# Attention scores of a macaron block on Trainium2: two PSUM banks per slot, or three banks with one head of the next slot computed early

## The reference

```python
def _L0_attn_ref(x, WQ, WK, WV, WO):          # x: (16, 256, 128), 16 heads, D_K = 8
    Q, K, V = (heads(WQ), heads(WK), heads(WV))
    score = jnp.einsum('bhqd,bhkd->bhqk', Q, K) / jnp.sqrt(jnp.asarray(D_K, x.dtype))
    score = score + mask                       # -inf above the diagonal
    score = score - jnp.max(score, axis=-1, keepdims=True)
    score = jnp.exp(score)
    score = score / jnp.sum(score, axis=-1, keepdims=True)
    out = jnp.einsum('bhqk,bhkd->bhqd', score, V)
    ...
    return out @ WO
...
x = x + 0.5 * _L0_ffn_ref(_layernorm(x, axis=-1), L0_ffn_gate_w, L0_ffn_w1, L0_ffn_w2, L0_ffn_w3)
x = x + _L0_attn_ref(_layernorm(x, axis=-1), L0_attn_WQ, L0_attn_WK, L0_attn_WV, L0_attn_WO)
x = x + 0.5 * _L0_ffn_ref(_layernorm(x, axis=-1), L0_ffn_gate_w, L0_ffn_w1, L0_ffn_w2, L0_ffn_w3)
```

## Time and profile before

| | |
|---|---|
| median of 3 runs | 566.49 us (564.69 to 567.13) |
| profiled execution | 565.05 us, its span 563.0 us |
| granted TensorE clock, mean | 0.993 of full speed |
| busy time of PE, DVE, ACT, POOL | 501.2, 373.7, 317.2, 267.9 us |
| score products (L1753) | 1024, mean 244 ns each |
| score maxima (L1322) | 128, mean 816 ns each |
| exponentials (L953) | 128, mean 813 ns each |

### The profile page before, as it was taken

How to read it: one execution, slowest core, us unless ns; L and a number is a source line. 1 busy time by engine, 2 the same in 40 slices (tenths; PEclk the granted TensorE clock), 3 DMA queues, 4 the chain that set the end, 5 groups by cost and what they waited for, 6 DMA issues and landing times.

```text
span 563.0 us, 19023 instructions
## 1 busy us (share of the span) xinstructions
PE 501.2 (89%) x7286; PEld 411.0 (73%) x7286; DVE 373.7 (66%) x995; ACT 317.2 (56%) x597; POOL 267.9 (48%) x325
## 2 busy tenths in 40 slices
PE   1689999999999788898889886888889999999995
PEld 1679998988889456565656554655579999999995
DVE  5656865324675789999898898776375532455665
ACT  4945654433335576767676765667744444445553
POOL 7967877612463323333431111565607601666662
PEclk9999999999999799999999999999999999999999
DMA  9971247786764314846212120311147755843222
GB/s 271 306 242 50 61 100 161 175 157 155 129 138 121 102 59 108 245 109 186 79 58 62 41 60 2 119 57 36 45 94 164 155 133 130 156 119 91 72 75 56
DMA packets 114661, 65.86 MB, mean 117 GB/s; under 512 B 51856, under 2 KB 108432, under 8 KB 114576
## 3 DMA queue, kind: packets, MB, share of 16 engines
q1 hardware_dynamic: 84400, 38.95, 27.0%
q0 software_dynamic: 6912, 14.17, 10.0%
q10 hardware_dynamic: 23264, 11.54, 8.3%
HBM read 18.88 MB, written 34.87 MB: 95 GB/s over the span
## 4 chain that ended last, share of the span: by engine, by line
PE 61%; DVE 20%; ACT 6%; DMA 5%; issue 4%; POOL 1%; SPq 1%; ACTq 0%; DVEq 0%; POOLq 0%
PE bank L1641 19%; PE bank L1522 10%; PE bank L1524 10%; PE bank L1523 10%; DVE negmax L1322 8%; ACT pt L953 3%; PE bank L1753 3%; PE bank L1534 2%; PE bank L1816 2%; PE bank L1783 2%; DMA yg<-sorted_y,row 2%; DVE X L1219 2%; PE bank L1831 1%; ACT r_xn L785 1%; ACT ot L933 1%
## 5 line engine op out<-in xcount | busy, mean ns | idle before, releaser
L689 POOL DMA_INDIRECT yg<-sorted_y,row x108 | 104.1, 964 | 141.7 <-PE bank L1641 45.7
L1210 DVE SCALAR_TENSOR_TENSOR pt<-bank,pt 128x512 f32<-128x512 f32 x122 | 84.3, 691 | 118.3 <-PE bank L1524 109.8
L953 ACT ACTIVATE pt<-bank 128x768 f32<-128x768 f32 x128 | 104.1, 813 | 72.2 <-PE bank L1792 71.7
L675 POOL DMA_INDIRECT sorted_x<-xs,row x108 | 106.5, 987 | 52.0 <-issue 22.5
L1641 PE MATMUL bank<-w,pt 128*128 (+1 forms) x976 | 130.0, 277 | 0.0
L1641 PEld LDWEIGHTS bank<-w,pt 128*128 128x128 f32 x976 | 118.6, 192 | 3.2
L1322 DVE TENSOR_REDUCE negmax<-bank 128x10 f32<-128x640 f32 x128 | 104.4, 816 | 17.1 <-PE bank L1770 15.3
L829 ACT ACTIVATE pt<-bank 128x512 f32<-128x512 f32 x122 | 72.8, 597 | 26.3 <-PE bank L1524 25.1
L837 ACT ACTIVATE yb<-bank 128x256 f32<-128x256 f32 x82 | 31.5, 384 | 79.5 <-PE bank L1641 72.9
L1753 PE MATMUL bank<-zc 63*64 63x64 f16 (+3 forms) x1024 | 43.0, 244 | 16.6 <-DVE negmax L1322 13.8
L1753 PEld LDWEIGHTS bank<-zc 63*64 63x64 f16 x1024 | 18.9, 105 | 43.6 <-DVE negmax L1322 29.3
(11 more groups left out here) (171 smaller groups left out, 1015.8 us busy)
## 6 DMA issues: line engine op xcount, KB each, us to landing
sorted_y<-yb ACTq DMA_DIRECT2D x82, 128.0 KB
sorted_x<-zeros SPq DMA_DIRECT2D x2, 2944.0 KB, 14.5
zc<-qk_rows SPq DMA_DIRECT2D x84, 64.0 KB
qk_rows<-qksplit SPq DMA_DIRECT2D x8, 512.0 KB, 2.8
sorted_x<-zeros SPq DMA_DIRECT2D x1, 2432.0 KB, 11.4
sorted_x<-zeros SPq DMA_DIRECT2D x1, 2176.0 KB, 10.3
X<-x_in SPq DMA_DIRECT2D x8, 256.0 KB, 5.1
zc<-w_up SPq DMA_DIRECT2D x8, 256.0 KB, 6.7
```

The lines of the kernel that those rows point to most:

```text
L675: ps.indirect_dma_start(out=sorted_x[s], out_offset=bass.IndirectOffsetOnAxis(ap=row[:, s, k, t:t + 1], axis=0), in_=xs[:, R0[s] + t, :], ...
L689: ps.indirect_dma_start(out=yg[:, a % D_YG, k, :], out_offset=None, in_=sorted_y[s], in_offset=bass.IndirectOffsetOnAxis(ap=row[:, s, k, t ...
L953: s_.activation(pt[:, hg, (u % 2) * 768:(u % 2 + 1) * 768].rearrange("p (a n) -> p a n", a=2), bank[:, B_ST:B_ST + 2, 0:384], ACT.Exp, sca ...
L1210: v_.scalar_tensor_tensor(hid[:, n % D_HID], bank[:, B_H3 + n % 2, :], 1.0 / WSCALE, silu[:, n % D_H], ALU.mult, ALU.mult).then_inc(prod_d ...
```

## The change

PE no longer writes the scores of a slot ahead in one piece. Three banks, 0, 1 and 2, hold scores; an even slot uses 0 and 1, an odd one 1 and 2. The transposed scores move from banks 2 and 3 to banks 3 and 4. The head whose bank the slot before does not use (`first_side`: head 0 in bank 0 for an even slot, head 1 in bank 2 for an odd one) is computed one slot earlier, behind the transposed scores (`score_first`); the other head, in bank 1, is computed where both were before (`score_second`). In the first slot of attention both stand together. Each part has four products and two masks, all on the two quarters of the array of one head. The loop over heads is taken out of the products, so that in the early slots, too, the four products of head 0 stand ahead of the four of head 1. The numbers of instructions and DMAs are the same, those of the other engines and their order too, except that VectorE's reduction reads banks 0 and 1 or banks 1 and 2.

```diff
-        B_S, B_ST, B_O = 0, 2, 5
+        B_S, B_ST, B_O = 0, 3, 5
...
+        def score_place(n, a):
+
+            return B_S + n % 2 + a
+
+        def first_side(n):
+
+            return n % 2
+
...
-            def row_max(b, q, k, b0=B_S):
+            def row_max(b, q, k, early=False):
+                n = PAIRS * b + k
+                b0 = B_EARLY if early else score_place(n, 0)
...
-            def score_products(b, q, u, G_z=None, b0=B_S):
+            def score_products(b, q, u, a, place, G_z=None):
...
-                pe.wait_ge(s_reduced, freed(PAIRS * b + u))
                 for n in range(2):
-                    for a in range(2):
-                        rows = slice(HALF * a, HALF * (a + 1) - 1)
-                        for g in range(2):
...
+                    rows = slice(HALF * a, HALF * (a + 1) - 1)
+                    for g in range(2):
...
+            def score_masks(a, place):
+
+                own = causal[side(a), :, HALF * a:HALF * (a + 1)]
+                for g in range(2):
+                    parts = bank[side(g), place, 0:S_COLS].rearrange("p (s k) -> p s k", k=HALF)
+                    last = t_.matmul(parts[:, g:PARTS:4 - g, :], one(a), own,
+                                     start=False, stop=True, skip_group_check=True)
+                return last
+
+            def score_first(b, q, u, G_z):
+
+                n = PAIRS * b + u
+                if n > PAIRS + AHEAD:
+                    pe.wait_ge(s_reduced, done(n - 2, D_S))
+                a = first_side(n)
+                score_products(b, q, u, a, score_place(n, a), G_z)
+                score_masks(a, score_place(n, a))
+
+            def score_second(b, q, u):
+
+                n = PAIRS * b + u
+                if n > PAIRS + AHEAD:
+                    pe.wait_ge(s_reduced, done(n - 1, D_S))
+                a = 1 - first_side(n)
+                score_products(b, q, u, a, score_place(n, a))
+                score_masks(a, score_place(n, a)).then_inc(s_ready, 1)
...
                     if ahead is not None:
-                        score_products(*ahead, G + 1 if ahead[1] % 2 == 0 else None)
-                        score_masks()
+                        if b == 0 and u == 0:
+                            score_first(*ahead, None)
+                        score_second(*ahead)
                     score_t_products(b, q, u)
                     score_t_masks()
+                    coming = score_bank(b, q, u + 1) if u + 1 < PAIRS else score_bank(b + 1, q + 1, 0)
+                    if coming is not None:
+                        score_first(*coming, coming[0] // 2 if coming[1] % 2 == 0 else None)
...
-                    score_products(slot // PAIRS, slot // PAIRS, slot % PAIRS, 0 if slot < PAIRS else None, B_EARLY)
-                    score_masks(B_EARLY)
+                    pe.wait_ge(s_reduced, freed(slot))
+                    for a in range(2):
+                        score_products(slot // PAIRS, slot // PAIRS, slot % PAIRS, a, B_EARLY + a,
+                                       0 if slot < PAIRS and a == 0 else None)
+                    for a in range(2):
+                        last = score_masks(a, B_EARLY + a)
+                    last.then_inc(s_ready, 1)
```

More of the change, by code:

```diff
@@ L1453, in first_groups @@
                 if slot is not None:
-                    row_max(slot // PAIRS, slot // PAIRS, slot % PAIRS, B_EARLY)
+                    row_max(slot // PAIRS, slot // PAIRS, slot % PAIRS, early=True)
                 if slot == PAIRS - 1:
@@ L1762, in one @@
                 return ident_b[side(a), side(a)]
-            def score_masks(b0=B_S):
-                for a in range(2):
-                    own = causal[side(a), :, HALF * a:HALF * (a + 1)]
-                    for g in range(2):
-                        parts = bank[side(g), b0 + a, 0:S_COLS].rearrange("p (s k) -> p s k", k=HALF)
-                        last = t_.matmul(parts[:, g:PARTS:4 - g, :], one(a), own,
-                                         start=False, stop=True, skip_group_check=True)
-                last.then_inc(s_ready, 1)
+            def score_masks(a, place):
[19 more added lines that the diff above has]
+                score_masks(a, score_place(n, a)).then_inc(s_ready, 1)
             def score_t_products(b, q, u):
```

12 lines of the change are left out of this document (6 added, 6 removed).

## The result

| | before | changed |
|---|---|---|
| median, same chip | 565.76 us (4 runs, 564.69 to 567.13) | 572.28 us (4 runs, 570.94 to 572.83) |
| profiled execution | 565.05 us, span 563.0 | 571.94 us, span 569.9 |
| granted TensorE clock, mean | 0.993 | 0.997 |

The ratio is 1.0123, 95% interval 1.0091 to 1.0156: slower by 1.2%, 6.5 us between the medians. The forecast was 571.5 us, with 565.5 to 578.5 and a chance of 0.65 for slower.

What follows compares the result with a forecast made beforehand. PE bounds the first FFN; in attention mostly VectorE, some slots PE. Terms 1.0 + 3.0 + 1.7 + 0.4 = 6.1 us on 565.05 give 571.2, stated as 571.5 us; range 565.5 to 578.5.

Steps and rivals of the forecast that it cites:

- the early slots: Twelve blocks between expert units: head 1's short products wait behind head 0's long ones, 0.08 us each, 1.0 us in all.
- the waits for the DMAs: Attention, slot u = 3 of every second sequence: `score_first` waits for `zc` ahead of projection and transposes, 1.7 us in all.
- array time of one head alone, a slot: Behind the transposed scores, `score_first` adds its own time on PE: 0.19 us for each of 116 slots.
- attention slots, with VectorE's other waits: Attention: `score_first` delays reach VectorE in 13 slots plus remainders, 3.0 us; the reciprocal's later transposes add 0.4 us.
- wait for the DMAs, last group: Last group: PE waits for `zc` first, projection and transposes follow, 1.1 us plus the part's own 0.2, 1.3 us.
- the same, fourth group: Fourth group: up to 1.1 us of new waiting for `zc`, partly hidden by VectorE's work; 0.4 us taken.
- Columns per quarter, not a price per matmul: Score blocks on the array: time follows columns on each quarter, so one head lasts as long as both, 0.22 us.
- the halves that end no sooner: `score_second` behind the wait: masks still start 0.16 us after its first product, VectorE 0.45 us after it; gain 0.
- Covered in most slots: Attention: PE's waits, ScalarE's copy or VectorE's other work hide most 0.19 us parts; 13 slots and remainders cost 3.0 us.
- VectorE's waits don't fall: Attention: VectorE's waits for score masks, 23 times and 11.1 us, should not shrink.
- The rival of a maximum that starts sooner: Attention: a shorter part behind the wait halves VectorE's 11.1 us of waiting, giving 561 us; chance 0.07.
- PE as the bound: Attention: parts costing 0.3 us exceed the cover and PE drags most slots, giving 580 us; chance 0.12.

Runs made afterwards that it cites:

- opposite halves and no early wait: Changed kernel with odd slots' banks swapped and a new half group's first head not sent ahead: 566.39 us, ratio 1.004 to the kernel before.
- opposite halves: Changed kernel with odd slots' banks swapped, so head 0 is always sent ahead: ratios to the kernel before 0.998, 0.9983 and 0.9946, all on slower chips.
- doubled part: Changed kernel with every `score_first` (four products, two masks) issued twice in a row: 580.38 us, ratio 1.0312 to the kernel before.

## Why the prediction was right

The forecast held, and its mechanism, the columns of each quarter and a wait moved ahead of other work, is the measured one. Of its terms, some were mis-sized and offset one another, and that the sum came out as close as it did is luck: the early slots were 0.9 us too high and the waits for the DMAs 1.2 too low. The two executions that were profiled also differ by 1.5 us ahead of the first maximum, in code that is the same. To separate them I compare the changed kernel with the last one above, opposite halves and no early wait: both traces have the same clock at the start of attention, which the kernel before's has not. The stretch in which attention starts, of before and, in the second fence, of opposite halves with no early wait:

```profile
182.00:195.00 13.00, 10.41 (x203) 6.81 (x201) 7.88 (x23) 7.22 (x12) 4.63 (x6) 0.74 0.42 113
```

```profile
184.00:197.00 13.00, 9.01 (x201) 6.71 (x203) 8.82 (x27) 7.45 (x12) 4.50 (x6) 1.00 0.47 135
```

The granted clock was 0.74 in one and 1.00 in the other, as in the changed kernel. Counted from the first of each, the 33rd maximum of before comes 0.6 us later than in the other trace and the 33rd exponential 0.85 us later. From first to last exponential the changed kernel takes 5.65 us more than opposite halves with no early wait.

| term | forecast | measured |
|---|---|---|
| array time of one head alone, a slot | 0.19 | 0.192 |
| early slots | 1.0 | 0.1 |
| attention slots, with VectorE's other waits | 3.0 + 0.4 | 2.8 |
| wait for the DMAs, last group | 1.3 | 2.2 |
| the same, fourth group | 0.4 | 0.65 |
| sum | 6.1 | 5.7 |

The measured terms of attention are steps in the distance between the maxima of the two kernels: 0.65 at the fourth group, 2.2 at the last, the rest in single steps of up to 0.3 us. They are a little small, since the kernel compared with still pays 0.2 to 0.5 us itself; against before at an equal clock attention grew by 5.9 to 6.1 us.

- *Columns per quarter, not a price per matmul* was right, by 0.192 us, by the halves that end no sooner, and by opposite halves, which fit beside one another. It also says what the alternative was: the other head's quarters stood empty beside each part. The working on record was weaker than its result: 160 ns for eight products, 60 for four masks and 170 for eight transposed products are 20, 15 and 21 ns each, which rules out a fixed price per matmul only by the masks. The doubled part does it: six matmuls on two quarters take the time of twelve on four. The Trainium skill's rule of about 81 ns for a matmul of 128 columns ("TensorE: Matmul & The Clock Gate", section "Back-to-back issue gap") does not hold for these quarters: an estimate by it gives the doubled part, six more pairs, 0.49 us, and it took 0.21. The page gives this figure for a stream of pairs and says nothing of quarters or places. The full products of 128 columns don't show it either, each with a weight load of its own: they stand 0.06 us apart (302.70 and 302.76 in the earlier trace rows).
- *The early slots* are the step that failed: "dispatch is in order: the long products of head 0 wait for the short ones on their quarters before head 1 may begin". They don't hold head 1 back: its short product starts 0.014 us after that of head 0, and the twelve blocks cost 0.08 us together in place of 1.0. In the changed slot above, too, a matmul of a free quarter starts ahead of one that stands before it in the program and waits for its own quarter. The price was also set too high in itself, since 64 to 128 columns at 2.4 GHz are 0.03 to 0.05 us and not 0.05 to 0.08. The same page of the Trainium skill says under "Step-by-step: what each phase is for" that matmuls stay in program order; for the starts on different quarters the trace disagrees (305.37 ahead of 305.39).
- *Covered in most slots* was right. 13 fully exposed slots and remainders were counted, 3.0 us, and the waits behind them 0.4; 2.8 were measured. The doubled part came out at 3.8 times the single one in slots 66 to 96, as going through the slots had given it. Over all of attention it did not: the doubled kernel takes 15.1 us more than opposite halves with no early wait, with the waits for the DMAs adding nothing, where 12.5 had been counted. That its whole time fell in the expected range is luck, since the lost wait offset this.
- *The wait for the DMAs* was right in place and too small in size. I had counted the projection and the transposes behind it, and 0.2 for the part; but nothing lies beside a part that waits by itself (0.32), VectorE's normalisation comes late too (0.16), and the transfer itself took 0.66 us longer from its issue than in the trace that I read.
- *VectorE's waits don't fall*, 11.1 us in both. The rival of a maximum that starts sooner is out. PE as the bound is out as well: it is found waiting for VectorE 60 times still.

What stays open: why the change costs nothing that can be measured on the slower chips. In slots 66 to 96 it costs the same 1.25 us there, so the array time is paid. One term is absent there: all waits for the DMAs between 195 and 400 us in the unedited changed kernel's trace are

```profile
PE bank L1761 <- DMA zc<-qk_rows: 0.4, 1, 0.4
```

and from the maximum of slot 111 to that of slot 112 are 1.93 or 1.94 us in it and in every other trace from such a chip. SP's issue stands 7.7 us ahead of the maximum of slot 111 there (381.40 and 389.10). So the last group's 2.2 us are not paid. That leaves some 3.5 us of the table unaccounted for. The rest of attention is full of gaps that belong to no wait, behind which a late part may be hidden, but no trace of the kernel before was taken on such a chip, and this was only argued. The two costs were also never taken away one at a time on a chip of the faster kind: there their sizes are read from where the steps stand.

## What to carry to other kernels

Work cut in two along quarters of the array is not half as long: ask for each piece which quarters it uses, and what stands beside it. If a piece is to go early, put it where the neighbour uses the other quarters, and leave it where it was when its data arrives late. When totals can't tell kernels apart, look for a stretch in which two traces of the same kernel agree, and compare the others there.

## What the runs showed of the hardware

- Matmuls on different quarters of the array did not start in the order of the program: transposed products whose quarters were free started at 305.37, ahead of score products at 305.39 that stand before them, and in an early slot head 1's short product started at 131.738, ahead of head 0's long one at 131.777.
- Six matmuls on two quarters (four products, two masks, 448 columns a quarter) took 0.21 us right behind six equal ones, as long as twelve on four quarters (0.22).
- The same program took 572 us on one chip and 603 on another, with gaps of PE of up to 1.1 us that end by nothing in the profile, and yet a stretch of 100 us ran alike on both (a delay of 19.2 us at its start and at its end).
- TensorE ran at its lower level (256 columns in 0.21 us) up to 42.62 us in one trace and 47.46 in another, in the same code. The view's 1.00 ahead of these times stands for no record; the spacing of equal matmuls tells the level.
